# A warm-up that runs beside the first norm, and 2 KB rows for the input and the output of a recurrent mixer gated by routed experts

## The chip, the cores and the metric

The kernel runs on one core of a Trainium2 chip. TensorE (PE) multiplies matrices out of SBUF into PSUM banks, VectorE (DVE) and ScalarE (ACT) do the elementwise work, GpSimd (POOL) and SyncE (SP) mostly issue DMAs. Engines wait for each other and for DMAs by semaphores. The metric is the device time of one execution in microseconds (us); lower is better. Times of the kernel before are the median, the lowest and the highest of three runs; the profile is of one further execution.

## The reference, cut to what matters

The input x has 16 sequences of 256 tokens with 128 channels each, 4096 tokens in all, in float32.

```
xn   = (x - mean) / sqrt(var + 1e-5)                      # over the 128 channels of a token
s    = mixer(xn)       # shift by one token, six 128x128 projections, a scan over the 256 tokens,
                       # group norm over 8 channels, a gate, an output projection
cur  = xn
for r in range(4):                                        # four rounds of a mixture of experts
    logits = cur @ Wg[r] + bg[r]                          # 4 experts, the best 2 get a softmax weight cw
    hmid   = gelu(cur @ W1[e] + b1[e])                    # 128 -> 512, for every e
    y      = hmid @ W2[e] + b2[e]                         # 512 -> 128
    cur    = cur + sum_e cw[e] * y[e]
out  = x + s * silu(cur)
```

Every step but the norm, the last product and the last sum works on channels as rows, that is on x transposed.

## The kernel before

**Layout.** The work is done in NB = 8 blocks of BLK = 512 tokens, two sequences each. The large tensors hold channels in partitions and tokens along them: `cur` [128, 4096] is the state of the expert rounds, `xn_t` the normed input of the mixer. x comes from HBM with tokens in partitions instead. `load_x(c)` (L220) brings block c as four tiles of 128 tokens: tile t, partition p holds token 128t + p, which gives DMA rows of 128 floats, 512 B. The same layout is used when x is read again for the last sum (`load_x_again`, L272), and for the output (`store`, L278, and the two halves of the last block at L307 and L478).

**Start.** SP issues the loads of x blocks 0 and 1, then the eight loads of W1 and W2 in turns, then x blocks 2 to 7. DVE takes statistics of blocks 0 and 1 (`norm_stats`, L508), and then a chain of 14 tiny instructions of 8 columns gives 1/std by Newton steps (`norm_spread`, `norm_root`). `link` (L487) raises the semaphore `dve_step` after an instruction whose result the next one reads, and makes DVE wait for it; that happens 15 times up to 1/std. Then DVE norms two tiles of block 0 (L773, raises `xn_first`), ACT the other two (`scale_block`, L357, raises `xn_ready`). Ahead of `scale_block(0)` ACT has four roundings of weights in its queue (L426 to L429), each of which waits for its load. PE turns the four tiles of block 0 by transposes with `turn_normed(0)` (L893): the stationary operand is the normed tile in `xn_st` (its memory is `o`), the moving one is the identity `ident`, and tile t lands in columns 128t to 128t + 127 of the bank `pb`. DVE splits the result in a high and a low part (`split_cur(0)`, L571 and L573), and PE begins `up(0)`, three matmuls of 512 columns for each of four banks (L887, L888, L891). ACT takes each bank by a GELU (L389).

**Warm-up.** PE has nothing to do until block 0 is normed. It runs WARM_UP = 52 transposes of the identity into a bank that nobody reads (L1012), and FILL = 4 more behind `turn_normed(0)` (L1015).

**Main part.** 128 steps (4 rounds, 8 blocks, 4 experts) follow. In each, PE does `up` of the next step and `down` of this one, 24 matmuls of 512 columns, and pieces of the mixer, of the router and of the norm of blocks 2 to 7 are put between by fixed tables of steps. POOL adds each expert's result to `cur` by an accumulating DMA (L329).

**End.** For blocks 0 to 6, once their last round is done, ACT and DVE form th = s·silu(cur) with channels in partitions, PE turns it back by `turn_product(b)` (L904, four transposes at L909, the stationary operand is a tile of `th`), DVE adds x (L762), and SP stores. The last block goes in two halves: two transposes each (L1053), two sums (L881), and one store from SP (L307) and one from ACT (L478).

Of the kernel before, what the change touches and what calls it, by code (L numbers as in the profile page):

```python
# [5 lines left out]
D = 128  # L6
# [15 lines left out]
RSQRT_SEED = float(0x5F3759DF)  # L22
WARM_UP, FILL = 52, 4
DMA = 16
# [45 lines left out]
def mixer_gated_experts(nc, x, proj_t, mixes, wout_t, chan_vecs, wg, bg, w1, b1, w2, b2, cw_scratch, out):  # L70
# [7 lines left out]
    with ExitStack() as ctx:  # L78
# [134 lines left out]
        def block_of(k):  # L213
            return slice(k % NB * BLK, (k % NB + 1) * BLK)

        block = ctx.enter_context(nc.Block())

        @block.sync
        def _(sp):
            def load_x(c):  # L220
                sp.dma_start(cur[:, block_of(c)].rearrange("p (t d) -> p t d", t=TPB),
                             x[c * BLK:(c + 1) * BLK, :].rearrange("(t p) d -> p t d", p=128)).then_inc(x_loaded[c], DMA)

# [48 lines left out]
            def load_x_again(b):  # L272
                if b >= 2:
                    sp.wait_ge(r_empty, r_jobs["end", b - 2] + 1)
                sp.dma_start(xr[:, b % 2, :].rearrange("p (t d) -> p t d", t=TPB),
                             x[b * BLK:(b + 1) * BLK, :].rearrange("(t p) d -> p t d", p=128)).then_inc(x_again[b % 2], DMA)

            def store(b):  # L278
                sp.wait_ge(r_empty, r_jobs["end", b] + 1)
                sp.dma_start(out[b * BLK:(b + 1) * BLK, :].rearrange("(t p) d -> p t d", p=128),  # L280
                             o[:, b % 2, :].rearrange("p (t d) -> p t d", t=TPB)).then_inc(stored[b % 2], DMA)

# [17 lines left out]
            for b in range(NB - 1):  # L300
# [3 lines left out]
                if END_TURN + 2 + b < TURNS:  # L304
                    spread_gates(END_TURN + 2 + b)
            sp.wait_ge(half_done, 1)
            sp.dma_start(out[(NB - 1) * BLK:(NB - 1) * BLK + BLK // 2, :].rearrange("(t p) d -> p t d", p=128),  # L307
                         o[:, 1, 0:BLK // 2].rearrange("p (t d) -> p t d", t=TPB // 2)).then_inc(last_stored, DMA)
# [23 lines left out]
        def _(act):  # L332
# [139 lines left out]
            for n in range(2):  # L472
# [4 lines left out]
            act.wait_ge(half_done, 2)  # L477
            act.dma_start(out[(NB - 1) * BLK + BLK // 2:NB * BLK, :].rearrange("(t p) d -> p t d", p=128),  # L478
                          o[:, 1, BLK // 2:BLK].rearrange("p (t d) -> p t d", t=TPB // 2)).then_inc(last_stored, DMA)
# [405 lines left out]
        def _(pe):  # L885
# [7 lines left out]
            def turn_normed(b):  # L893

                if b == 0:
                    pe.wait_ge(xn_first, 1)
                else:
                    pe.wait_ge(p_empty, b)
                pe.wait_ge(xn_ready, b + 1)
                for t in range(TPB):  # L900
                    ins = nc.tensor.transpose(pb[:, t * D:(t + 1) * D], xn_st[:, b % 2, t * D:(t + 1) * D], ident[:, :])
                ins.then_inc(p_full, 1)

            def turn_product(b):  # L904

                pe.wait_ge(z_ready, b + 1)
                pe.wait_ge(r_empty, r_jobs["end", b])
                for t in range(TPB):
                    ins = nc.tensor.transpose(rb[:, t * D:(t + 1) * D], th[:, b % 2, t * D:(t + 1) * D], ident[:, :])  # L909
                ins.then_inc(r_full, 1)  # L910
# [100 lines left out]
            for _ in range(WARM_UP):  # L1011
                nc.tensor.transpose(rb[:, 0:D], ident[:, :], ident[:, :])  # L1012
            turn_normed(0)
            for _ in range(FILL):
# [34 lines left out]
            for n in range(2):  # L1049
                pe.wait_ge(half_z, n + 1)  # L1050
                for t in range(2):
                    col = n * HALF + t * D
                    ins = nc.tensor.transpose(hb[n][:, t * D:(t + 1) * D], th[:, (NB - 1) % 2, col:col + D], ident[:, :])  # L1053
                ins.then_inc(half_turned, 1)
# [33 lines left out]
```

## Time and profile before

| what | value |
|---|---|
| three timed runs | 809.54 us median (808.49 to 809.75) |
| the profiled execution's own time | 809.94 us |
| its span, first to last instruction | 808.1 us |
| PE / DVE / ACT / POOL busy | 98% / 88% / 81% / 14% |
| mean granted clock of TensorE | 0.995 of full |

The span and the device time of the same execution differ by 1.8 us, which lies before the first and behind the last instruction. Idle time of an engine that is not the bottleneck costs nothing; the busy share of PE counts modelled ends of overlapping matmuls, so it says that PE rarely stops and not how fast it goes. Where PE's speed matters, the granted clock of the stretch and the distance from one matmul's start to the next are read.

### The profile page before, as it was taken

The page shows a single profiled execution, that of the slowest core. Times are in us where ns is not written, and L with a number is a line of the kernel's source. Part 1 is how long each engine was busy: PE and PEld are TensorE (multiplying, and loading weights), DVE is VectorE, ACT ScalarE, POOL GpSimd, SP SyncE. Part 2 cuts the span into 40 slices and gives each one's busy share as a digit, 9 for nine tenths or more (in the row PEclk, how much of TensorE's full clock was granted, in tenths as well). Part 3 has the DMA queues.
Part 4 walks back from the last instruction along what each step waited for, and adds up shares of the span by engine and source line. Part 5 has one row for each costly group of instructions (what it writes and reads, how often), then busy time and mean ns, then how long its engine had stood idle before and what let it go on. Part 6 is the DMA issues. An engine that isn't in the chain of part 4 may idle for free.

```text
span 808.1 us, 10652 instructions
## 1 busy us (share of the span) xinstructions
PE 794.2 (98%) x3668; PEld 639.0 (79%) x3668; DVE 712.0 (88%) x1328; ACT 652.7 (81%) x912; POOL 114.5 (14%) x135
## 2 busy tenths in 40 slices
PE   7999999999999999999999999999999999999997
PEld 6778788887888878888788887888788887777885
DVE  5989888889998989889998899898989898989887
ACT  6899888877888877888787887788788887778775
POOL 0021111111111111111111101111111111011110
PEclk9999999999999999999999999999999999999998
DMA  9444462432532416333264322544235343264532
GB/s 256 121 84 123 81 183 54 105 92 40 147 83 59 104 27 158 93 72 73 40 145 105 92 40 56 134 108 96 41 90 133 92 117 77 40 172 105 130 66 52
DMA packets 44468, 78.50 MB, mean 97 GB/s; under 512 B 6656, under 2 KB 23552, under 8 KB 40448
## 3 DMA queue, kind: packets, MB, share of 16 engines
q0 software_dynamic: 18144, 33.04, 24.3%
q1 hardware_dynamic: 25136, 44.64, 16.5%
q8 instruction: 29, 0.48, 0.2%
q10 hardware_dynamic: 1136, 0.16, 0.1%
q14 instruction: 23, 0.19, 0.1%
HBM read 40.34 MB, written 2.36 MB: 53 GB/s over the span
## 4 chain that ended last, share of the span: by engine, by line
PE 91%; DVE 3%; DMA 3%; ACT 1%; issue 1%; SPq 0%; DVEq 0%; ACTq 0%; POOLq 0%
PE h_bank L887 14%; PE h_bank L891 14%; PE y_bank L952 14%; PE y_bank L948 14%; PE y_bank L947 14%; PE h_bank L888 14%; DMA cur<-tmp 2%; PE p_bank L887 2%; PE p_bank L891 2%; PE p_bank L888 2%; PE r_bank L986 1%; PE p_bank L917 1%; DMA cw_b<-in_w 1%; DVE g_lo L624 1%; ACT g L389 1%
## 5 line engine op out<-in xcount | busy, mean ns | idle before, releaser
L389 ACT ACTIVATE g<-h_bank,b_c 128x512 f32<-128x512 f32 x512 | 330.0, 682 | 75.0 <-PE h_bank L891 73.4
L624 DVE TENSOR_TENSOR g_lo<-g,g_hi 128x1024 fp32r<-128x1024 f32 x256 | 308.4, 1221 | 64.9 <-ACT g_hi L393 64.2
L393 ACT ACTIVATE g_hi<-g 128x1024 fp32r<-128x1024 f32 x256 | 271.9, 1062 | 8.1
L329 POOL DMA_DIRECT2D cur<-tmp x126 | 113.3, 899 | 680.9 <-DVE tmp L638 546.3
L887 PE MATMUL h_bank<-cur_hi,w_hi 128*128 128x512 f32 x512 | 206.5, 403 | 0.6 <-ACT g L389 0.4
L891 PE MATMUL h_bank<-cur_lo,w_hi 128*128 128x512 f32 x512 | 203.9, 398 | 0.0
L888 PE MATMUL h_bank<-cur_hi,w_lo 128*128 128x512 f32 x512 | 202.8, 396 | 0.0
L947 PE MATMUL y_bank<-g_hi,w_hi 128*128 128x512 f32 x508 | 201.1, 396 | 0.0
L948 PE MATMUL y_bank<-g_hi,w_lo 128*128 128x512 f32 x508 | 200.6, 395 | 0.0
L952 PE MATMUL y_bank<-g_lo,w_hi 128*128 128x512 f32 x508 | 139.3, 396 | 0.0
L891 PEld LDWEIGHTS h_bank<-cur_lo,w_hi 128*128 128x128 f32 x512 | 96.4, 188 | 23.4 <-DVE cur_lo L573 0.2
L887 PEld LDWEIGHTS h_bank<-cur_hi,w_hi 128*128 128x128 f32 x512 | 97.0, 189 | 21.6 <-issue 2.2
L947 PEld LDWEIGHTS y_bank<-g_hi,w_hi 128*128 128x128 f32 x508 | 95.4, 188 | 23.5 <-issue 0.8
L948 PEld LDWEIGHTS y_bank<-g_hi,w_lo 128*128 128x128 f32 x508 | 95.4, 188 | 23.2
L952 PEld LDWEIGHTS y_bank<-g_lo,w_hi 128*128 128x128 f32 x508 | 95.4, 188 | 22.9
L888 PEld LDWEIGHTS h_bank<-cur_hi,w_lo 128*128 128x128 f32 x512 | 96.7, 189 | 19.1
L638 DVE SCALAR_TENSOR_TENSOR tmp<-y_bank,b_c,cw_b 128x512 f32<-128x512 f32 x127 | 94.4, 743 | 1.3 <-DMA cur<-tmp 1.2
L672 DVE SCALAR_TENSOR_TENSOR xm<-xx,mix,xn_t 128x256 f32<-128x256 f32 x96 | 42.0, 479 | 0.6
L680 DVE TENSOR_TENSOR xm_lo<-xm,xm_hi 128x512 fp32r<-128x512 f32 x48 | 33.2, 692 | 1.7
L887 PE MATMUL p_bank<-xm_hi,pj_hi 128*128 128x256 f32 x96 | 27.3, 285 | 0.0
L891 PE MATMUL p_bank<-xm_lo,pj_hi 128*128 128x256 f32 x96 | 27.2, 283 | 0.0
L888 PE MATMUL p_bank<-xm_hi,pj_lo 128*128 128x256 f32 x96 | 27.0, 282 | 0.0
(133 smaller groups left out, 497.5 us busy)
## 6 DMA issues: line engine op xcount, KB each, us to landing
cur<-tmp POOLq DMA_DIRECT2D x126, 256.0 KB, 3.4
cw_b<-cw_scratch SPq DMA_DIRECT2D x31, 1024.0 KB, 5.1
cur<-in_x SPq DMA_DIRECT2D x8, 256.0 KB, 5.6
xn_t<-cur SPq DMA_DIRECT2D x8, 256.0 KB, 2.9
xr<-in_x SPq DMA_DIRECT2D x8, 256.0 KB, 3.5
out<-o SPq DMA_DIRECT2D x7, 256.0 KB, 2.4
cw_b<-in_w SPq DMA_DIRECT2D x4, 256.0 KB, 6.2
cw_b<-cw_scratch SPq DMA_DIRECT2D x1, 768.0 KB, 5.4
```

Of the source, the lines that this page charges most:

```text
L329: pool.dma_start(cur[:, block_of(s // E)], tmp[:, s % 2, :], accum_op=ALU.add).then_inc(summed, DMA)
L389: nc.scalar.activation(g[:, gb, ft * BLK:(ft + 1) * BLK], hb[ft][:, :], ACT.Gelu_apprx_tanh, bias=b1_c[:, e * FT + ft:e * FT + ft + 1]).th ...
L393: nc.scalar.activation(g_hi[:, gb, h], g[:, gb, h], ACT.Copy).then_inc(g_hi_done, 1)
L624: nc.vector.tensor_tensor(g_lo[:, gb, h], g[:, gb, h], as_f32(g_hi[:, gb, h]), ALU.subtract).then_inc(g_lo_done, 1)
L638: nc.vector.scalar_tensor_tensor(out=tmp[:, s % 2, :], in0=yb[s % 2][:, :], scalar=b2_c[:, e:e + 1], in1=cw_b[:, q, e * BLK:(e + 1) * BLK] ...
L672: last = nc.vector.scalar_tensor_tensor(out=xm[:, n, :], in0=xx[:, :], scalar=mix[:, k:k + 1], in1=xs[:, 1:LEN + 1], op0=ALU.mult, op1=ALU ...
L887: nc.tensor.matmul(out_ap, w_hi, v_hi, start=True, stop=False)
L888: nc.tensor.matmul(out_ap, w_lo, v_hi, start=False, stop=False)
L891: return nc.tensor.matmul(out_ap, w_hi, v_lo, start=False, stop=True)
L947: nc.tensor.matmul(yb[b][:, :], w2_hi[:, e * FT + ft, :], hi, start=(ft == 0), stop=False)
L948: nc.tensor.matmul(yb[b][:, :], w2_lo[:, e * FT + ft, :], hi, start=False, stop=False)
L952: last = nc.tensor.matmul(yb[b][:, :], w2_hi[:, e * FT + ft, :], g_lo[:, b, ft * BLK:(ft + 1) * BLK], start=False, stop=(ft == FT - 1))
```

## The change

There are two parts.

**Tokens per partition.** `by_partition` and `by_tile` give every DMA of x and of the output another split: partition p of a block holds tokens 4p to 4p + 3, so that one DMA row is 2 KB. In the last block, which is stored in halves, partition p holds two neighbouring tokens of each half, 1 KB rows. Tile t of a block now holds the tokens t, t + 4, t + 8 and so on. So that `cur` and `xn_t` keep tokens in order, `turn_normed` writes each tile into every fourth column of the bank (every second column of a half in the last block), and `turn_product` and the last turns read every fourth (second) column of `th` as stationary operand. `tokens_of` gives these slices. The four transposes of a block, and their sizes, stay.

**Warm-up.** The 52 transposes become 36, then 15 pairs, each behind a wait for one of DVE's 15 steps up to 1/std, then 3 behind the wait for `xn_first`: 69 in all. The 4 of FILL stay.

```diff
-WARM_UP, FILL = 52, 4
+WARM_UP, FILL = 36, 4
+
+ROOT_CHAIN = 15
...
+        def by_partition(b, rows):
+            if b < NB - 1:
+                return rows.rearrange("(p t) d -> p t d", t=TPB)
+            return rows.rearrange("(n p t) d -> p n t d", n=2, t=TPB // 2)
+
+        def by_tile(b, ap):
+            if b < NB - 1:
+                return ap.rearrange("p (t d) -> p t d", t=TPB)
+            return ap.rearrange("p (n t d) -> p n t d", n=2, t=TPB // 2)
+
+        def tokens_of(b, t):
+
+            if b < NB - 1:
+                return slice(t, BLK, TPB)
+            n, i = t // (TPB // 2), t % (TPB // 2)
+            return slice(n * HALF + i, (n + 1) * HALF, TPB // 2)
...
-                sp.dma_start(cur[:, block_of(c)].rearrange("p (t d) -> p t d", t=TPB),
-                             x[c * BLK:(c + 1) * BLK, :].rearrange("(t p) d -> p t d", p=128)).then_inc(x_loaded[c], DMA)
+                sp.dma_start(by_tile(c, cur[:, block_of(c)]),
+                             by_partition(c, x[c * BLK:(c + 1) * BLK, :])).then_inc(x_loaded[c], DMA)
...
-                sp.dma_start(out[b * BLK:(b + 1) * BLK, :].rearrange("(t p) d -> p t d", p=128),
-                             o[:, b % 2, :].rearrange("p (t d) -> p t d", t=TPB)).then_inc(stored[b % 2], DMA)
+                sp.dma_start(by_partition(b, out[b * BLK:(b + 1) * BLK, :]),
+                             by_tile(b, o[:, b % 2, :])).then_inc(stored[b % 2], DMA)
...
-                    ins = nc.tensor.transpose(pb[:, t * D:(t + 1) * D], xn_st[:, b % 2, t * D:(t + 1) * D], ident[:, :])
+                    ins = nc.tensor.transpose(pb[:, tokens_of(b, t)], xn_st[:, b % 2, t * D:(t + 1) * D], ident[:, :])
...
-                    ins = nc.tensor.transpose(rb[:, t * D:(t + 1) * D], th[:, b % 2, t * D:(t + 1) * D], ident[:, :])
+                    ins = nc.tensor.transpose(rb[:, t * D:(t + 1) * D], th[:, b % 2, tokens_of(b, t)], ident[:, :])
...
             for _ in range(WARM_UP):
+                nc.tensor.transpose(rb[:, 0:D], ident[:, :], ident[:, :])
+            for n in range(ROOT_CHAIN):
+                pe.wait_ge(dve_step, n + 1)
+                for _ in range(2):
+                    nc.tensor.transpose(rb[:, 0:D], ident[:, :], ident[:, :])
+            pe.wait_ge(xn_first, 1)
+            for _ in range(3):
                 nc.tensor.transpose(rb[:, 0:D], ident[:, :], ident[:, :])
             turn_normed(0)
...
-                    ins = nc.tensor.transpose(hb[n][:, t * D:(t + 1) * D], th[:, (NB - 1) % 2, col:col + D], ident[:, :])
+                    ins = nc.tensor.transpose(hb[n][:, t * D:(t + 1) * D], th[:, (NB - 1) % 2, tokens_of(NB - 1, 2 * n + t)],
+                                              ident[:, :])
```

`load_x_again` changes like `load_x`, and the two half stores of the last block change from `"(t p) d -> p t d"` to `"(p t) d -> p t d"` with t = 2.

PE's queue at the start of the program, before. L1012 is the warm-up, L901 the turn of block 0, L1015 FILL, L887 to L891 the first bank of `up(0)`.

```order
L1012 MATMUL r_bank<-ident 128x128 [waits made]
L1012 MATMUL r_bank<-ident 128x128 x51
L901 MATMUL p_bank<-ident,o 128x128 [waits xn_ready,xn_first]
L901 MATMUL p_bank<-ident,o 128x128 x3
L1015 MATMUL r_bank<-ident 128x128 x4
L887 MATMUL h_bank<-cur_hi,w_hi 128x512 [waits cur_split,w1_low]
```

The same place now (the pair at L1036 stands 15 times, two of them are shown; lines have moved by 20 and more).

```order
L1032 MATMUL r_bank<-ident 128x128 [waits made]
L1032 MATMUL r_bank<-ident 128x128 x35
L1036 MATMUL r_bank<-ident 128x128 [waits dve_step]
L1036 MATMUL r_bank<-ident 128x128
L1036 MATMUL r_bank<-ident 128x128 [waits dve_step]
L1036 MATMUL r_bank<-ident 128x128
...
L1039 MATMUL r_bank<-ident 128x128 [waits xn_first]
L1039 MATMUL r_bank<-ident 128x128 x2
L921 MATMUL p_bank<-ident,o 128x128 [waits xn_ready,xn_first]
L921 MATMUL p_bank<-ident,o 128x128 x3
L1042 MATMUL r_bank<-ident 128x128 x4
L907 MATMUL h_bank<-cur_hi,w_hi 128x512 [waits cur_split,w1_low]
```

The turn of block 0 stands behind 69 transposes instead of 52, the last 33 of them behind waits for DVE.

SP's queue at the start, before; the shape is partitions x tiles x floats of a row.

```order
L221 DMA cur<-in_x 128x4x128 x2
L225 DMA cw_b<-in_w 128x512 x2
L228 DMA th<-in_w 128x4x128
L225 DMA cw_b<-in_w 128x512
```

And now.

```order
L241 DMA cur<-in_x 128x512 x2
L245 DMA cw_b<-in_w 128x512 x2
L248 DMA th<-in_w 128x4x128
L245 DMA cw_b<-in_w 128x512
```

The order of SP's queue is the same; a load of x is 128 rows of 512 floats where it was 512 rows of 128.

## Rows read from the trace of the kernel before

**Rows 1.** The page, span and PE's busy share.

```profile
span 808.1 us, 10652 instructions
...
PE 794.2 (98%) x3668; PEld 639.0 (79%) x3668; DVE 712.0 (88%) x1328; ACT 652.7 (81%) x912; POOL 114.5 (14%) x135
```

**Rows 2.** Chain that ended last, 0 to 19 us: start, us, what.

```profile
3.26 6.56 DMA cw_b<-in_w
...
10.47 0.78 ACT o L365 x2
...
11.39 0.64 PE p_bank L901 x4
...
12.05 0.70 DVE cur_hi L571
...
14.51 0.43 PE h_bank L887
...
16.39 0.23 PE h_bank L887
...
17.09 0.45 PE p_bank L901 x4
...
18.68 0.58 ACT g L389
```

**Rows 3.** Timeline of ACT, 5 to 22 us: start, us, instruction, idle before.

```profile
9.85 0.63 ACT L345 ACTIVATE w_hi<-cw_b 128x512 fp32r<-128x512 f32 x1
...
14.25 0.58 ACT L374 ACTIVATE cur<-p_bank 128x512 f32<-128x512 f32 x1
14.73 0.67 ACT L389 ACTIVATE g<-h_bank,b_c 128x512 f32<-128x512 f32 x1
15.73 0.69 ACT L389 ACTIVATE g<-h_bank,b_c 128x512 f32<-128x512 f32 x1 [0.33 <-PE h_bank L891]
```

**Rows 4.** Timeline of DVE, 5 to 15 us.

```profile
5.97 0.87 DVE L513 BATCH_NORM_STATS2 stats<-cur 128x6 f32<-128x128 f32 x4 [1.32 <-DMA cur<-in_x]
...
9.95 0.17 DVE L533 SCALAR_TENSOR_TENSOR shift<-mean,rstd 128x8 f32<-128x8 f32 x1
...
12.78 0.69 DVE L573 TENSOR_TENSOR cur_lo<-p_bank,cur_hi 128x512 fp32r<-128x512 f32 x1
```

**Rows 5.** Timeline of PE, 0 to 14 us.

```profile
1.77 7.56 PE L1012 MATMUL r_bank<-ident 128*128 128x128 f32 x52 [1.77 <-POOL ident L318]
11.39 0.63 PE L901 MATMUL p_bank<-ident,o 128*128 128x128 f32 x4 [2.06 <-ACT o L365]
```

**Rows 6.** Windows: busy of each engine, granted clock, DMA share, GB/s last.

```profile
4.00:5.00 1.00, 1.00 (x6) 1.00 (x5) 0.65 (x4) 1.00 (x1) 0.00 (x0) 1.00 0.88 109
5.00:6.00 1.00, 1.00 (x11) 1.00 (x10) 0.03 (x1) 0.31 (x2) 0.00 (x0) 1.00 0.81 276
...
12.00:13.00 1.00, 0.83 (x6) 0.46 (x3) 0.91 (x2) 1.00 (x4) 0.00 (x0) 0.52 1.22 290
13.00:14.00 1.00, 1.00 (x3) 0.76 (x4) 1.00 (x3) 1.00 (x3) 0.00 (x0) 0.50 1.23 290
...
5.20:9.60 4.40, 4.13 (x38) 3.89 (x36) 3.18 (x20) 1.89 (x4) 0.00 (x0) 1.00 1.08 330
```

**Rows 7.** The page, DMA issues: KB each, median us to landing.

```profile
out<-o SPq DMA_DIRECT2D x1, 128.0 KB, 1.9
```

**Rows 8.** Waits of PE, whole span: waited for, us in total, times, longest.

```profile
PE r_bank L909 <- DVE th L737: 4.1, 3, 1.5
```

**Rows 9.** Timeline and window of the end.

```profile
804.12 1.12 PE L1053 MATMUL h_bank<-ident,th 128*128 128x128 f32 x4 [2.56 <-DVE th L753]
804.94 0.76 DVE L881 TENSOR_TENSOR o<-h_bank,xr 128x256 f32<-128x256 f32 x2 [0.54 <-PE h_bank L1053]
...
803.00:806.00 3.00, 1.12 (x4) 0.67 (x4) 2.15 (x7) 0.42 (x1) 0.00 (x0) 0.66 0.00 0
```

More of the change, by code:

```diff
@@ L274, in load_x_again @@
                     sp.wait_ge(r_empty, r_jobs["end", b - 2] + 1)
-                sp.dma_start(xr[:, b % 2, :].rearrange("p (t d) -> p t d", t=TPB),
-                             x[b * BLK:(b + 1) * BLK, :].rearrange("(t p) d -> p t d", p=128)).then_inc(x_again[b % 2], DMA)
+                sp.dma_start(by_tile(b, xr[:, b % 2, :]),
+                             by_partition(b, x[b * BLK:(b + 1) * BLK, :])).then_inc(x_again[b % 2], DMA)
             def store(b):
                 sp.wait_ge(r_empty, r_jobs["end", b] + 1)
-                sp.dma_start(out[b * BLK:(b + 1) * BLK, :].rearrange("(t p) d -> p t d", p=128),
-                             o[:, b % 2, :].rearrange("p (t d) -> p t d", t=TPB)).then_inc(stored[b % 2], DMA)
+                sp.dma_start(by_partition(b, out[b * BLK:(b + 1) * BLK, :]),
+                             by_tile(b, o[:, b % 2, :])).then_inc(stored[b % 2], DMA)
             copy_block(0)
@@ L306, in _ @@
             sp.wait_ge(half_done, 1)
-            sp.dma_start(out[(NB - 1) * BLK:(NB - 1) * BLK + BLK // 2, :].rearrange("(t p) d -> p t d", p=128),
+            sp.dma_start(out[(NB - 1) * BLK:(NB - 1) * BLK + BLK // 2, :].rearrange("(p t) d -> p t d", t=TPB // 2),
                          o[:, 1, 0:BLK // 2].rearrange("p (t d) -> p t d", t=TPB // 2)).then_inc(last_stored, DMA)
@@ L477, in _ @@
             act.wait_ge(half_done, 2)
-            act.dma_start(out[(NB - 1) * BLK + BLK // 2:NB * BLK, :].rearrange("(t p) d -> p t d", p=128),
+            act.dma_start(out[(NB - 1) * BLK + BLK // 2:NB * BLK, :].rearrange("(p t) d -> p t d", t=TPB // 2),
                           o[:, 1, BLK // 2:BLK].rearrange("p (t d) -> p t d", t=TPB // 2)).then_inc(last_stored, DMA)
@@ L1051, in _ @@
                 for t in range(2):
-                    col = n * HALF + t * D
-                    ins = nc.tensor.transpose(hb[n][:, t * D:(t + 1) * D], th[:, (NB - 1) % 2, col:col + D], ident[:, :])
+                    ins = nc.tensor.transpose(hb[n][:, t * D:(t + 1) * D], th[:, (NB - 1) % 2, tokens_of(NB - 1, 2 * n + t)],
+                                              ident[:, :])
                 ins.then_inc(half_turned, 1)
```

## The prediction, written before the changed kernel ran

> **What bounds the kernel now.** I read the page first: PE is busy for 98% of 808.1 us [rows 1]. So in the main part nothing but PE's own work counts, and a change that leaves the matmuls alone can only win at the start, at the end, or where PE is seen to wait. The waits of PE give just one such place in between, 4.1 us over three turns of a finished block at L909 [rows 8]; it waits there for DVE's product, whose inputs come from the accumulating DMAs.
>
> Then I read the chain of the start. It runs through the loads of W1 until 9.8 us, through ACT's fourth rounding (9.85) and its first two normed tiles (10.47), to PE's turn of block 0 at 11.39, DVE's split at 12.05, `up(0)`, and ends up on ACT, whose third GELU at 18.68 releases PE [rows 2]. Three things stand out. DVE has 1/std and the shift at 9.95 + 0.17 = 10.12 [rows 4], before ACT is free, so ACT and the weight loads bind and not DVE's chain. From 9.85 on ACT works without a gap, save 0.33 us at 15.73 where it waits for PE [rows 3]. And PE idles for 2.06 us between warm-up and turn [rows 5], after which its granted clock reads 0.52 and 0.50 of full from 12 to 14 us, the lower of the two levels (1.2 GHz) [rows 6]; a matmul of 512 columns takes 0.43 us there and 0.23 us later [rows 2].
>
> **Warm-up, PE.** At the full clock four turns take 0.45 us, 0.11 each [rows 2]. At half the clock I take twice that, 0.22, as the big matmuls do (0.43 against 0.23). The 52 fit this: PE's records per us go from 6 to 11 between the windows 4 to 5 and 5 to 6 [rows 6], so the step lies near 5.2 us; (5.2 - 1.77) / 0.22 = 16 at 0.22, then 36 at 0.11 = 4.0, together 7.4 of 7.56 us [rows 5]. Now there are 69: 16 at 0.22 (3.4 us) and 53 at 0.11 (5.8 us), so PE's queue reaches the turn at 1.77 + 9.2 = 11.0 us at the earliest. The 36 end near 7.4. The first of DVE's 15 steps comes right behind the statistics, at 5.97 + 0.87 = 6.84, the last near 9.95 [rows 4], 0.22 apart, and a pair takes 0.22 too, so PE trails DVE closely and hardly waits. The gap of 2.06 us is gone, PE is busy up to the turn, and I expect the clock to stay at the higher level. What is queued behind these waits is the turn of block 0 alone; it begins at 11.0 instead of 11.39, -0.37, if ACT's tiles are there.
>
> What is that worth? DVE's split moves with the turn: the low part ends at 12.78 + 0.69 - 0.37 = 13.1. `up(0)` starts at 12.5, waits for the low part, and at 0.23 per matmul its second bank is ready near 14.0, long before ACT asks. So ACT's gap of 0.33 closes, with some hundredths of others, 0.4 us in all. From 18.68 on PE follows ACT, so 0.4 us is what the clock gives, and not the 0.2 us on each of ten matmuls at the lower level: ACT takes over as the bound.
>
> The Trainium skill, "TensorE: Matmul & The Clock Gate", Part 4 (PE-mode transpose), says that transposes do not count as PE activity for the clock in the way matmuls do. The trace disagrees: with nothing but transposes running, PE's records per us went from 6 to 11 and the clock of 5.2 to 9.6 us is 1.00 [rows 6]. By that rule the longer warm-up would hold nothing; this is the second rival below.
>
> **2 KB rows, loads at the start.** A load of x in 512 B rows runs at 290 GB/s where it is alone (13 to 14 us), while the stretch 5.2 to 9.6 us, mostly 2 KB rows of W1, reads 330 [rows 6]. For 256 KB that is 0.90 against 0.79 us, 0.11 per load, and two stand ahead of the weights: 0.2 us is the lower bound for how much sooner the weights land. Above: between 4 and 5 us the queues moved only 109 GB/s at a DMA share of 0.88 [rows 6], so the small packets of the second load (landed 5.97, [rows 4]) drag there; if blocks 0 and 1 passed at 330 GB/s from the first packet, the second would be in up to 2 us sooner. But ACT's use of it is capped: its copy of block 0 at 14.25 [rows 3] waits for the split, 13.1, so 1.15 us is the upper bound. I take 0.7, the middle, since I see both the drag and no reason that it goes in full. Then ACT's fourth rounding starts at 9.15, its two tiles are ready near 10.6, the turn starts at 11.0, where PE's queue arrives, and ACT reaches its copy at 13.55, behind the split. ACT's chain is 0.7 + 0.4 = 1.1 us earlier at 18.68, and PE with it for the rest of the run. Bounds: 0.6 to 1.55.
>
> **2 KB rows, middle.** Seven stores and eight second loads of x get cheaper for the DMA engines by 0.11 us each, on a queue with slack. They share the engines with the accumulating DMAs that PE's three waits (4.1 us, [rows 8]) hang on: fewer packets help, larger ones make the other queue wait longer for its turn. I take 0, with 0.5 us either way.
>
> **End.** The half store lands 1.9 us after issue [rows 7]. With 1 KB rows 128 KB gain at most 0.06 us by the rates above; I take 0.05. The clock is at 0.66 on the mean of 803 to 806 us [rows 9]: the last four turns, at 804.12, run at the lower level, 0.82 us before DVE's first sum. If the end shifts by 1.1 us some of this may run before the clock falls: 0 to 0.4 us, of which I take 0.15.
>
> **Strided turns.** This is the part that I can't read from the trace. 32 turns write every fourth PSUM column (28 in the running stream), 28 + 4 read every fourth or second column of `th`. No row shows a strided operand on PE. Below: nothing, because a turn takes 0.11 us for 128 columns and a matmul 0.23 us for 512 [rows 2], so a turn streams at half the rate per column that PE and PSUM manage, which leaves room for an access to twice as many lines. Above: half speed, 0.22 instead of 0.11, as at the low clock, so 0.11 on each of 64, 7.0 us (3.5 for writes alone, 3.5 for reads alone). I take 0, by that spare rate.
>
> The Trainium skill, "Advanced Engine Details and Errata", Memory Cachelines, says of PSUM that "Any non-contiguous AP significantly slows down matmuls", as its lines hold two floats, and of SBUF that one access per 16-byte line costs. A step of four floats is one access per line in both. No run here shows it. By that rule the writes and the reads would both slow, 7.0 us by the bound above.
>
> **Sum.** -1.1 (start) - 0.05 - 0.15 (end) = -1.3 us against the profiled execution, 809.94 to 808.6. The median of the timed runs is 0.4 us lower than that execution, so I forecast 808.2 us.
>
> **Rivals.**
> First, strided turns are slow. It decides from 0.05 us per turn (64 x 0.05 = 3.2, less 1.3, is beyond 1.6). If one side, writes or reads, goes at half speed: +3.5 - 1.3, 811.7 us; both: 815.2. For it speaks that nothing in the kernel so far strides on PE, against it the spare rate of a turn. It is slower than before.
> Second, the clock still falls near 12 us, because ACT's tiles come late, or warm-up transposes don't hold it. Then PE runs ten matmuls at 0.43 and bounds the start; only the turn's 0.37 is kept, plus 0.1 at the end: 809.1 us.
> Third, the warm-up itself is late. If the clock rises later than at 5.2 us in an execution, more of the 69 take 0.22: 16 more of them put the turn at 12.8, 1.4 us after 11.39, so the time is about 0.5 us above before, 810.0. The 52 of before would have been done by 11.1.
> Fourth, the drag on the second load was the small rows' doing and goes in full, and the end gains its 0.4: 1.55 + 0.45 = 2.0 us, 807.5.
>
> **Chances.** About 0.2%, 1.6 us, is what a measurement of this kernel can tell from no change. The forecast 0.35 (808.2, its own range 807.6 to 808.9), the fourth 0.22, the second 0.09, the third 0.06, strided turns 0.28. Faster by over 1.6 us: the fourth and a quarter of the forecast's, 0.31. Slower: the strided turns and a little, 0.29. Within: 0.40. The range runs from 807.2 to 812.5; it holds the forecast, the second and third, the fourth, and strided turns on one side only, and leaves out half speed on both sides.
>
> **What would show it.** PE's timeline: transposes without a gap above 0.3 us from 1.77 to about 11.0, then the turn; a clock of 1.00 in the windows from 12 to 16 us; if the gap stays away and the clock still falls, the warm-up step is wrong. DVE's second statistics start by 0.5 us or more before 5.97, and ACT's fourth rounding near 9.15; if it stays at 9.6 or later, the DMA step is wrong. ACT's third GELU of `up(0)`, at 18.68 in the chain, comes near 17.6. The chain's row for four turns at the full clock reads 0.45 us if strides are free, and up to 0.9 if not, for blocks 1 to 7, and likewise at the seven turns of the products. PE's waits at the products stay near 4.1 us. The forecast is wrong if turns slow by 0.05 us or more each, or if the start gains less than 0.6 us.

## The result: 812.06 us, slower by 0.4%

The changed kernel takes 812.06 us (median of 6, 811.45 to 813.66). The kernel before took 809.43 us in the median on the same chip (6 runs, 808.49 to 809.75). The ratio is 1.0038, with a 95% interval of 1.0027 to 1.0050; it follows the means of the runs, and the medians lie 2.6 us, 0.3%, apart. The forecast was 808.2 us and faster; the time lies in the range of 807.2 to 812.5, but on the other side of the kernel before. Single executions that ran far longer as a whole (one each in e5, in e16 and in the runs of the kernel before beside e13 to e16) are left out of the medians and ratios, and their traces are not read.

The profiled execution took 811.45 us, 1.5 us more than that of before (809.94), and its span is 1.5 us longer (809.65 against 808.14). The page of the changed kernel, beside [rows 1]:

```profile
span 809.7 us, 10686 instructions
...
PE 796.4 (98%) x3685; PEld 641.6 (79%) x3685; DVE 711.6 (88%) x1328; ACT 652.2 (81%) x912; POOL 114.5 (14%) x135
...
DMA packets 35637, 78.52 MB, mean 97 GB/s; under 512 B 6656, under 2 KB 12032, under 8 KB 31616
...
xr<-in_x SPq DMA_DIRECT2D x8, 256.0 KB, 2.8
out<-o SPq DMA_DIRECT2D x7, 256.0 KB, 2.0
```

The DMA part of the change does what it says: there are 35,637 packets where there were 44,468, a second load of x lands in 2.8 us instead of 3.5, and a store in 2.0 instead of 2.4. The kernel is slower all the same. Laying the starts of PE's matmuls of both traces side by side (after minus before) says where:

```
at us    +us    place (times of the kernel before)
 11.4   +0.92   first turn of block 0
 15.5   -0.08   third bank of up(0); +0.02 at 694, behind the first turns of products
716.8   +1.2    PE stops for ACT's GELU
719.9   +1.6    turn of a finished product
795.3   +1.9    behind the last turns of products
804.1   +1.9    first half turn
804.6   +1.75   third half turn; span +1.5
```

So there are four readings: the start, the stretch 702 to 722 us, the turns and the end.

**The start.** PE's timeline of the changed kernel, as in [rows 5] (start, us, instruction, idle before):

```profile
1.77 7.10 PE L1032 MATMUL r_bank<-ident 128*128 128x128 f32 x36 [1.77 <-POOL ident L338]
8.70 3.44 PE L1036 MATMUL r_bank<-ident 128*128 128x128 f32 x30
11.98 0.49 PE L1039 MATMUL r_bank<-ident 128*128 128x128 f32 x3
12.30 0.60 PE L921 MATMUL p_bank<-ident,o 128*128 128x128 f32 x4
```

The gap is gone, but the 36 took 7.10 us where I had 5.6, and the turn starts at 12.30. The windows (PE, PEld, DVE, ACT, POOL, granted clock, DMA share, GB/s; compare [rows 6]):

```profile
5.00:6.00 1.00, 1.00 (x7) 1.00 (x6) 0.47 (x3) 0.13 (x1) 0.00 (x0) 1.00 0.65 209
...
12.00:13.00 1.00, 1.00 (x12) 1.00 (x11) 0.06 (x1) 1.00 (x4) 0.00 (x0) 1.00 1.07 373
13.00:14.00 1.00, 0.56 (x5) 0.35 (x3) 0.97 (x2) 1.00 (x3) 0.00 (x0) 1.00 1.05 385
```

Between 5 and 6 us PE still does 7 transposes per us, not 11: in this execution the clock came to its full level at 7.85 us, against 5.22 before. (The column of the granted clock reads 1.00 here all the same: the trace's record of the clock begins only when it rises, so before that PE's rate has to be read.) From 12 to 14 us it is 1.00 where it was 0.52 and 0.50, so the longer warm-up does hold it. The loads of x run at 373 and 385 GB/s against 290. DVE and ACT, as in [rows 3, 4]:

```profile
5.53 0.88 DVE L533 BATCH_NORM_STATS2 stats<-cur 128x6 f32<-128x128 f32 x4 [1.21 <-DMA cur<-in_x]
...
9.50 0.17 DVE L553 SCALAR_TENSOR_TENSOR shift<-mean,rstd 128x8 f32<-128x8 f32 x1
...
9.89 0.63 ACT L365 ACTIVATE w_hi<-cw_b 128x512 fp32r<-128x512 f32 x1
...
15.01 1.33 ACT L409 ACTIVATE g<-h_bank,b_c 128x512 f32<-128x512 f32 x2
```

The second block of x is in 0.44 us sooner (5.53 against 5.97), but ACT's fourth rounding starts at 9.89, no sooner than the 9.85 of before: ACT, which bound here before, got nothing from the loads, and PE's 69 transposes, without a gap up to the turn, now come in last. The gap of 0.33 us between its first two GELUs is gone, and the late turn has taken it back.

**The stretch 702 to 722 us.** The chain of waits of the changed kernel, 711 to 724 us:

```profile
703.51 7.92 DMA cur<-tmp
...
711.96 4.73 DMA cur<-tmp
...
717.21 3.56 DMA cur<-tmp
720.78 0.68 DVE th L757
...
721.50 0.75 PE r_bank L929 x4
```

and that of the kernel before, which the prediction had not read:

```profile
703.55 7.45 DMA cur<-tmp
...
711.53 3.55 DMA cur<-tmp
...
715.62 3.55 DMA cur<-tmp
719.16 0.69 DVE th L737
...
719.90 0.66 PE r_bank L909 x4
```

Here the path runs over three accumulating DMAs in a row, not over PE. The first takes 0.47 us longer, the second 1.18 us, the third the same; less the 0.04 by which the stretch began sooner, that is the whole 1.6 us at the turn. The first of them stands beside another broadcast, issued at 704.0, a store and a second load of x. What stands beside the second is seen in SP's queue. The timeline of the changed kernel:

```profile
706.22 0.32 SPq L283 DMA_DIRECT2D cw_scratch<-cw  x1
711.96 0.86 POOL L349 DMA_DIRECT2D cur<-tmp  x1 [7.59 <-DMA cur<-tmp]
712.72 0.32 SPq L290 DMA_DIRECT2D cw_b<-cw_scratch  x1
716.71 0.63 ACT L444 ACTIVATE th<-cur 128x512 f32<-128x512 f32 x1 [4.20 <-DMA cur<-tmp]
```

and of the kernel before:

```profile
706.26 1.14 SPq L263 DMA_DIRECT2D cw_scratch<-cw  x1
711.53 0.86 POOL L329 DMA_DIRECT2D cur<-tmp  x1 [7.12 <-DMA cur<-tmp]
712.69 0.33 SPq L270 DMA_DIRECT2D cw_b<-cw_scratch  x1
715.11 0.64 ACT L424 ACTIVATE th<-cur 128x512 f32<-128x512 f32 x1 [2.65 <-DMA cur<-tmp]
```

The gates' save (L283, before L263) is issued at 706.2 in both, and the broadcast of the gates (1 MB in 8 KB rows), which waits in SP's queue for the save to land, at 712.7 in both. The accumulate, issued when the one before it has landed, comes 0.43 us later in the changed kernel. So the broadcast follows it after 0.76 us instead of 1.16. The records of the DMA packets show what that does. In the kernel before, 101 of the accumulate's 128 packets of 2 KB start before 714 us and the others before 715, and the 8 KB packets begin behind 714. In the changed kernel 49 start before 714 us, 47 before 715, and 32 later, when 8 KB packets (42 in that us, 324 ns each) already hold the engines. The sum lands late, so does the tanh (wait 4.20 instead of 2.65), and PE stops twice:

```profile
PE r_bank L929 <- DVE th L757: 4.4, 3, 1.9
...
PE h_bank L907 <- ACT g L409: 1.3, 2, 0.9
```

These are PE's waits (us in total, times, longest); [rows 8] had 4.1 for the first, and the wait of 0.9 us for the GELU is new.

**The turns.** Read by form, the instructions of the two turn lines (ns, least/median/most):

```profile
L929 PEld LDWEIGHTS r_bank<-ident,th x28: 195/211/220, 642.2 to 797.0; 128*128 128x128 f32 x28
L929 PE MATMUL r_bank<-ident,th x28: 270/285/386, 642.4 to 797.1; 128*128 128x128 f32 x28
...
L921 PE MATMUL p_bank<-ident,o x32: 270/272/273, 12.3 to 84.4; 128*128 128x128 f32 x32
```

and of the product's turns before:

```profile
L909 PEld LDWEIGHTS r_bank<-ident,th x28: 137/141/142, 642.3 to 795.1; 128*128 128x128 f32 x28
L909 PE MATMUL r_bank<-ident,th x28: 270/273/328, 642.5 to 795.2; 128*128 128x128 f32 x28
```

Writing every fourth PSUM column costs nothing: 272 ns, one per 0.109 us as before. Reading every fourth column of `th` costs something: the weight load takes 211 ns instead of 141, and the turns follow each other at 0.122 us instead of 0.109. That is 28 x 0.013 = 0.4 us.

**The end**, as in [rows 7, 9]:

```profile
806.00 0.96 PE L1079 MATMUL h_bank<-ident,th 128*128 128x128 f32 x4 [2.56 <-DVE th L773]
806.65 0.78 DVE L901 TENSOR_TENSOR o<-h_bank,xr 128x256 f32<-128x256 f32 x2 [0.37 <-PE h_bank L1079]
...
805.00:806.00 1.00, 0.00 (x0) 0.00 (x0) 1.00 (x4) 0.39 (x1) 0.00 (x0) 1.00 0.00 0
806.00:807.00 1.00, 0.96 (x4) 0.64 (x4) 0.63 (x3) 0.00 (x0) 0.00 (x0) 0.78 0.00 0
```

DVE's sum starts 0.65 us behind the first half turn instead of 0.82: part of the turn still runs at the full clock. The forecast had 0.15 for this, and it is 0.17. The half stores land in 1.7 us instead of 1.9, for which the forecast had 0.05. Together the end is 0.4 us shorter: 1.9 us late before the half turns, 1.5 in the span.

### The profile page after: what moved, and what is told of

Same layout as the page of the kernel before. It is cut to its first block, busy times and chain, and to the rows that moved or that the text cites. A ratio compares the mean times of both kernels' runs of the same rounds, so it can differ in the third digit from the quotient of the medians.

```text
span 809.7 us, 10686 instructions
## 1 busy us (share of the span) xinstructions
PE 796.4 (98%) x3685; PEld 641.6 (79%) x3685; DVE 711.6 (88%) x1328; ACT 652.2 (81%) x912; POOL 114.5 (14%) x135
## 2 busy tenths in 40 slices
DMA packets 35637, 78.52 MB, mean 97 GB/s; under 512 B 6656, under 2 KB 12032, under 8 KB 31616
## 4 chain that ended last, share of the span: by engine, by line
PE 92%; DVE 3%; DMA 2%; ACT 1%; issue 1%; POOL 0%; DVEq 0%; POOLq 0%; ACTq 0%
PE y_bank L972 14%; PE h_bank L911 14%; PE h_bank L907 14%; PE y_bank L968 14%; PE y_bank L967 14%; PE h_bank L908 14%; DMA cur<-tmp 2%; PE p_bank L907 2%; PE p_bank L911 2%; PE p_bank L908 2%; PE r_bank L1006 1%; PE r_bank L1032 1%; PE p_bank L937 1%; DVE g_lo L644 1%; ACT g L409 1%
```

## The experiments

Ratios are to the kernel before, run in turn with each on the same chip; they follow the means, so the medians can give a ratio that is some hundredths of a per cent away. Five rounds unless it says otherwise.

**Halves of the change.** The warm-up alone:

```diff
-WARM_UP, FILL = 52, 4
+WARM_UP, FILL = 36, 4
+            for n in range(ROOT_CHAIN):
+                pe.wait_ge(dve_step, n + 1)
+                (two transposes)
+            pe.wait_ge(xn_first, 1), and three more
```

> The kernel before with the new warm-up alone (36, 15 pairs behind DVE's steps, 3), old layout. Theory A (the loss sits in the DMAs around the finished blocks, near 704 to 720 us): no loss here, within 0.4 us of before, 809.0 to 809.8; the part of the chain behind 20 us is unchanged. Theory B (the 69 transposes put the first turn late when the clock rises late, as in the profile after, 7.85 us and a turn at 12.3): 0.3 to 1.5 us slower than before.

Measured: 809.26 against 809.28 us, 1.0000 [0.9991, 1.0009]. The profiled execution took 808.43 us, and here the clock rose at 5.02 us:

```profile
10.92 0.60 PE L902 MATMUL p_bank<-ident,o 128*128 128x128 f32 x4
...
8.96 0.63 ACT L346 ACTIVATE w_hi<-cw_b 128x512 fp32r<-128x512 f32 x1
...
4.00:5.00 1.00, 1.00 (x6) 1.00 (x5) 0.70 (x4) 1.00 (x1) 0.00 (x0) 1.00 0.83 158
```

In this execution everything came as predicted for the clock: the 36 transposes took 5.71 us, the turn came at 10.92, the third GELU at 17.22. And the fourth rounding came at 8.96 with the 512 B rows of before, whose queues moved 158 GB/s between 4 and 5 us instead of 109. When the loads at the start let ACT begin this rounding differs by 0.9 us from execution to execution with the same rows.

The layout alone, all of the diff but the warm-up:

> The changed kernel with the old warm-up of 52. Theory A: as slow as the changed kernel, 811.5 to 812.5, with PE's waits near 717 us 1.0 to 1.5 us longer than before. Theory B: 809 to 809.8 (a load 0.4 us sooner, strided reads +0.4 us), the changed kernel's loss gone.

Measured: 812.93, 1.0051 [1.0033, 1.0068]. The whole loss is in the layout. Next its two sides: 2 KB rows in the first loads with strided PSUM writes (e3), and the rest: second loads, stores and strided reads of `th` (e4).

> Only the first loads of x in 2 KB rows, with the strided PSUM writes of the turns; second loads, stores, turns of the products and warm-up as before. Theory A: no loss, 809.0 to 809.6; turns of blocks 1 to 7 still 0.45 us per four. If strided writes cost: 3.5 us slower.

Measured: 809.08, 1.0000 [0.9992, 1.0009]; turns at 0.109 us. The input's side costs and gives nothing.

> Only the second loads of x and the stores in 2 KB rows, with the strided reads of th in the turns; first loads and warm-up as before. Theory A: the loss is here, 811 to 812, of it 0.4 us from strided reads (0.12 instead of 0.11 us per turn) and the rest at the wait near 717 us. Theory B: 809.5 to 810, only the reads' 0.4 us.

Measured: 812.6, 1.0035 [1.0021, 1.0049]. All of it is in the output's side. The chain of e4 has the second accumulate at 5.78 us:

```profile
711.36 5.78 DMA cur<-tmp
...
717.66 3.54 DMA cur<-tmp
```

PE's stop there is 2.1 us, and behind it the granted clock falls (e4's windows; columns as above):

```profile
718.00:719.00 1.00, 0.59 (x2) 0.50 (x3) 0.00 (x0) 0.97 (x3) 0.52 (x1) 0.75 0.00 0
719.00:722.00 3.00, 2.34 (x7) 1.34 (x5) 1.94 (x3) 2.97 (x5) 0.00 (x0) 0.51 0.52 90
```

e2's profiled execution (815.38 us) shows the same from 722.7 to 726.1 us, beside a fall at the start as in the kernel before. This is a second price of the late sum, paid in some executions only; in the profiled execution of the change the clock stayed up. How far it lifts the median of the change is not shown. The traces in which the clock falls once have a mean granted clock of 0.995 or 0.996, those in which it does not 0.998 or 0.999; of the six executions of the change two have 0.995 and less, and the two at the median have 0.997.

**Rows or reads?** e5 keeps the 2 KB rows of e4 and turns `th` by contiguous columns; e6 keeps the strided reads with the rows of before. Both leave out the right order of the output's tokens.

```diff
e5 -  ... th[:, b % 2, tokens_of(b, t)]      e6 -  by_tile / by_partition in load_x_again, store, last stores
   +  ... th[:, b % 2, t * D:(t + 1) * D]       +  "(t p) d -> p t d" as before
```

> Second loads and stores in 2 KB rows, but the turns of the products read th contiguously, so that rows of the output stand at other tokens (the order of the output is left out). Theory A1 (2 KB packets of SP's queue set the accumulating DMA near 711 us against the broadcast of the gates): all but 0.4 us of the loss of e4 is here, 811.5 to 812.5; tanh near 715 us waits 4 to 5.4 us for its accumulate instead of 2.7. Theory A2 (the strided reads of th make the loss): 809.0 to 809.6.

> DMAs as before, only the turns of the products read th in steps of four, two in the last block (the order of the output is left out). Theory A1: 0.3 to 0.5 us over before (28 turns at 0.122 instead of 0.109 us), 809.5 to 809.9. Theory A2: 811.5 to 812.5.

Measured: e5 811.5, 1.0036 [1.0023, 1.0048]; e6 811.05, 1.0026 [1.0017, 1.0035]. The rows alone make a loss as large as e4's, within the intervals. That the reads also seem to make 2.1 us did not fit e6's own trace, in which the turns cost 0.4 us and the span is 807.3; so it was tried again (e15). The kernel of e5 was run once more for its trace:

> The kernel of e5 once more, for a trace (the order of the output is left out): tanh of block 3 waits 4 us or more for its accumulate, the broadcast is issued 0.6 to 0.9 us behind the accumulate instead of 1.16, and turns of the products stay at 0.109 us; 811 to 812.5.

Measured, one run: 812.1 us, span 810.3, turns at 0.109 us, in its chain the second accumulate at 4.93 us, and a clock that falls at 721.9 us for 3.4 us. The rows do it without any strided read.

**The broadcast held back.** If the 8 KB packets between those of the accumulate are the cause, the change with the broadcast issued behind the accumulate must lose nothing:

```diff
+                if k == 29:
+                    sp.wait_ge(summed, DMA * 112)
                 sp.dma_start(cw_b[:, q, rest], line[rest].partition_broadcast(128)).then_inc(cwb_ready[q], DMA)
```

> The changed kernel, with one wait more on SP: the broadcast of the gates of turn 29 starts only when the accumulate that the tanh of block 3 waits for has landed (summed at 112). Theory A1: the loss goes, 808.8 to 810.0; tanh near 715 us waits 2.9 us or less, the clock does not fall there. If the delay is not from that collision: no change, 811.5 to 812.7, or slower if the broadcast becomes late itself.

Measured: 809.57 (11 runs, 809.16 to 809.9), 1.0007 [0.9998, 1.0016]. Its chain and SP's queue:

```profile
711.42 3.29 DMA cur<-tmp
...
714.74 0.64 ACT L446 ACTIVATE th<-cur 128x512 f32<-128x512 f32 x1 [2.99 <-DMA cur<-tmp]
714.78 0.32 SPq L292 DMA_DIRECT2D cw_b<-cw_scratch  x1
```

The accumulate lands in 3.29 us, the tanh comes at 714.74, the GELU's wait of 0.9 us is gone, and with it the loss: the medians lie 0.6 us above the kernel before on the same chip (809.57 against 808.97) where the change's lay 2.6 above. Of the 0.6 the strided reads make 0.4. None of the 11 executions has a mean clock under 0.997. One wait of one DMA for another, everything else as in the change, so it is shown that the loss hangs on the broadcast beside the second accumulate. The first accumulate still takes 8.15 us here.

**Stores or loads?** With three rounds each, the kernel before with 2 KB rows in the stores alone, or in the second loads alone (the order of tokens in the output is left out):

> The kernel before with only the stores of the output in 2 KB (1 KB in the last block) rows; second loads and turns as before (the order of the output is left out). By the collision theory each of the two, store and second load, brings the broadcast nearer to the accumulate by about half: 1.16 us apart becomes 0.95, and the loss lies between: 809.5 to 811.5.

> The kernel before with only the second loads of x in 2 KB rows (the order of the output is left out). The second load's packets are the last of SP's queue ahead of the gates' save, so if only one of the two matters it is this one: 810.5 to 812, and e13 at 809.3. If both count by half: 809.5 to 811.5.

Measured: stores 811.39, 1.0021 [1.0011, 1.0031]; loads 810.79, 1.0015 [1.0006, 1.0024]. Their chains have the second accumulate at 4.00 and 3.86 us instead of 3.53 to 3.56, so each brings on a part of the collision. That is 0.3 to 0.5 us, and with the stores the first accumulate is 0.2 to 0.5 us longer too; the medians lie 2.2 and 1.6 us above before. Most of it is the second price. In both profiled executions PE's stop at the turn of the product is 1.87 us, where it is 1.5 to 1.7 us in before, e1 and e3, and behind it the clock falls for 3.4 us. e14's window (columns as above):

```profile
720.00:723.00 3.00, 3.00 (x10) 2.25 (x9) 2.93 (x6) 2.39 (x4) 0.86 (x1) 0.53 0.00 0
```

Laid beside e3, whose clock stays up, e14's matmuls are 0.1 us late when this turn begins, 1.6 us late at 723.4 us, and 1.7 at the end. 8 of e14's 10 executions and 7 of e13's 8 have a mean clock of 0.996 or less.

The two differ in how they bring the broadcast nearer. With the stores the first accumulate takes 7.97 us (old rows: 7.45 to 7.74), and the broadcast follows the second after 0.86 us; with the loads it takes 7.48, but the broadcast comes sooner, 9.0 us behind the first accumulate's issue instead of 9.1 to 9.4, and follows the second after 1.01. The lengths of the two accumulates in the kernels without a held broadcast (us), by the chain, with the gap from the second's issue to the broadcast's:

```
kernel                          first          gap            second
before, e1, e3, e6, e8, e15     7.45 to 7.74   1.16 to 1.18   3.53 to 3.56
e14 (2 KB in the loads)         7.48           1.01           3.86
e13 (2 KB in the stores)        7.97           0.86           4.00
e2 (2 KB in both)               7.82           0.80           4.50
after                           7.92           0.76           4.73
e12                             7.99           0.74           4.93
e4                              8.04           0.69           5.78
```

The second accumulate grows as the gap shrinks, without an exception. With the old rows the first accumulate differs by 0.3 us from trace to trace too, but the broadcast moves with it and the gap stays.

**The reads again**, with the new warm-up:

> Strided reads of th as in e6, with the new warm-up of 36 + 30 + 3 (the order of the output is left out). If strided reads cost only what the trace shows, 0.4 us: 809.3 to 809.9 and a span 0.4 us over that of e1. If they cost the 2 us of e6's median: 811 or more. A clock that falls at the start in e6 (5 of 11 at a mean of 0.995) can't fall here.

Measured: 809.69, 1.0003 [0.9994, 1.0013], spans 807.85 in the median against 807.4. The strided reads cost some 0.4 us, as their rows say. The chain has the accumulates at 7.71, 3.56 and 3.56 us, as before: reads do not touch them. So e6's 2.1 us are not the reads'. Its six executions with a mean clock of 0.997 or 0.998 have a median span of 807.5 us, against 807.2 for the 25 such executions of the kernel before beside it, which is about what the reads cost. The rest is of two kinds: five of its 11 executions have a mean clock of 0.995, as those in which the clock falls once, and its times lie 2.6 us above their spans in the median instead of 1.8. Why e6 had more of both than e15 is open. (In e2 and e4 the distance to the span is also up to 2.8 us.)

**A shorter warm-up.** 18 instead of 36, on e1:

```diff
-WARM_UP, FILL = 36, 4
+WARM_UP, FILL = 18, 4
```

> The kernel before with the new warm-up, 18 transposes ahead of the 15 pairs instead of 36. Theory W (the 69 transposes arrive late, near 12.3 us, in the executions where the clock rises late, and in time where it rises early; that is why the warm-up alone gave nothing in the median): 0.5 to 1.0 us faster than before in the median, 808.3 to 808.8, and a narrower spread. If it is not the length: 809.2 as with 36.

Measured: 809.26 against 808.97, 1.0010 [1.0001, 1.0018]. With the clock up at 6.12 us the turn came at 11.17, not much before that of e7 (6.18, 11.49), and DVE and ACT bind again: no gain. The profiled execution took 810.99 us, and its clock fell too, at 719.5 us for 3.4 us, behind a stop of 1.81 us:

```profile
719.00:723.00 4.00, 3.65 (x11) 3.07 (x12) 3.93 (x8) 3.35 (x5) 0.86 (x1) 0.57 0.00 0
```

Its DMAs are those of the kernel before, so the fall in the middle does not need the 2 KB rows. 3 of its 11 executions have a mean clock of 0.995, and 1 of e1's 11 has 0.996.

**Holding the broadcasts in the other kernels.** If the kernel before also pays for the crowd, a wait before broadcasts 28 and 29 should gain there (e9), with the warm-up and the input's rows (e10), and in the change (e11):

```diff
+                if k in (28, 29):
+                    sp.wait_ge(summed, DMA * (k + 83))
```

> The kernel before, with the broadcasts of the gates of turns 28 and 29 held until the accumulates 111 and 112 have landed. If the crowd of DMAs costs time before the change too (tanh waits 2.65 us there, PE 1.5 us at 720): accumulate 111 lands near 707 instead of 711, PE's wait at 720 shrinks by 0.5 to 1.5 us, no execution with the clock fallen there; 808.0 to 808.6. If that wait has another cause: 808.9 to 809.3, no change.

> New warm-up, first loads in 2 KB rows, old second loads and stores, and both broadcasts held as in e9. Sum of the parts that gained or cost nothing: e9's time less 0.3 to 0.8 us from the start, 807.4 to 808.3; if start and crowd gain nothing, 809.0.

> The changed kernel with both broadcasts held. By the collision theory the 2 KB rows cost nothing once nothing collides: 0.4 us (strided reads) above e10, 808.0 to 809.2, and under e7's 809.6. If 2 KB rows hurt elsewhere: as e7 or above.

Measured against 810.02: e9 810.1, 1.0003 [0.9994, 1.0012]; e10 809.51, 0.9995 [0.9986, 1.0004]; e11 810.0, 1.0001 [0.9993, 1.0010]. Nothing is gained. e9's chain says why:

```profile
703.49 3.25 DMA cur<-tmp
...
707.27 8.10 DMA cur<-tmp
```

Without the broadcast beside it the first accumulate takes 3.25 us instead of 7.45. But that broadcast, issued at 706.8 us now, stands beside the second, which takes 8.10 us instead of 3.55, and DVE begins the product at 719.45 us instead of 719.16. PE's wait at the products falls from 4.1 to 2.9 us, and a new one of 0.9 us appears at the mixer's projections, for `xm_hi`, which DVE makes behind the product. The three together also say what the 2 KB rows cost once the broadcasts are held: e11 lies 0.5 us above e10, and the strided reads alone make 0.4 of it.

**The best of it**: input rows, warm-up of 18, broadcast 29 held, output as before.

> What gained or cost nothing, together: first loads in 2 KB rows, warm-up of 18 + 30 + 3, old second loads and stores, the broadcast of turn 29 held as in e7. 0.3 to 1.0 us faster than before if start and clock gains add up; equal if the held broadcast costs what they bring.

Measured: 809.0 against 809.2, 0.9997 [0.9988, 1.0006]. No version beats the kernel before by what can be measured.

## Why the prediction was wrong, step by step

**The step that failed is "2 KB rows, middle"**, taken at 0 with 0.5 us either way. I had named the effect, that larger packets make the other queue wait longer, and its size on the accumulate beside the store and the load is 0.47 us, at the bound that I gave. (Between traces with the same old rows this accumulate differs by 0.3 us, so 0.47 is not all the rows' doing.) What the step left out is the next one: an accumulate that is issued 0.4 us later meets the broadcast of the gates, whose own time did not move, and takes 1.18 us more. Together 1.6 us in the profiled execution, and about 1.5 more where the clock falls behind the stop (e14 beside e3). That the broadcast is the second part's cause is shown (e7), that the rows of stores and loads bring it on as well (e12, e13, e14). Why the first accumulate takes longer beside 2 KB rows than beside 512 B rows is not shown. [rows 8] showed that PE waits at the products; the chain of waits at 703 to 720 us, which I did not read, shows that for 16 us the path is three accumulates in a row, so that what delays one of them is paid in full.

**Warm-up**: the mechanism was right. The clock stays at its higher level (1.00 in the windows from 12 us on, and none of the seven traces with the new warm-up shows a fall at the start), and it rose at 7.85 us after nothing but transposes. The Trainium skill ("TensorE: Matmul & The Clock Gate", Part 4) says that transposes do not count as PE activity in the way matmuls do; these traces disagree. By the rule the longer warm-up would have held nothing. What the old warm-up loses was read from one trace: of the nine traces with it only three (before, e2, e9) show the fall near 12 us, so the gain of 0.4 us was there to be had in a part of the executions. What was mis-sized is the time at which the clock rises. I took 5.2 us from one execution; the same warm-up gives:

```
kernel   clock up   turn of block 0   third GELU
e1         5.02         10.92           17.22
e7         6.18         11.49           17.81
e11        7.11         11.94           18.24
e10        7.34         12.05           18.37
e15        7.59         12.18           18.48
after      7.85         12.30           18.61
```

The turn comes 0.49 us later for each us of late clock, since transposes take 0.22 instead of 0.11 us until then: this is the third rival's mechanism, to which I gave 0.06. Five of these six traces show it. Its price was too high: with the turn at 12.30 the third GELU comes at 18.61, where the rival had a time 0.5 us above before for a turn at 12.8. Before had its third GELU at 18.68 with a clock that rose early and fell again, and over its 23 executions beside e1 the spans lie at 806.4 to 807.6 us (13, mean clock 0.997 or more, median 806.9) or at 807.4 to 808.8 (10, mean clock 0.995 or 0.996, as where the clock falls once). The new warm-up takes away most of the second group, and a late turn lengthens the first: e1's ten executions with the higher clock have a median span of 807.45. Median for median, nothing.

**Loads at the start**, -0.7: mis-sized. The second load is in 0.44 us sooner in the profiled execution, and that is mostly luck: the six traces with the new rows at the start have 5.29 to 5.73 us for the second statistics (median 5.65), the ten with the old ones 5.25 to 5.98 (median 5.77). ACT's fourth rounding comes at 9.11 to 10.08 us with the new rows and at 8.96 to 9.85 with the old ones, 9.6 in the median of both. The drag at 4 to 5 us that I charged half to the small rows differs between executions of the same rows (109 GB/s in before, 158 in e1). e3 puts the whole step at 0.0 with 0.7 us either way.

**Strided turns**: writes at 0, right. Reads at 0, too low by 0.4 us; the upper bound of 3.5 was far off, and the first rival did not come, although its number for one side (811.7) is near the result. The Trainium skill's rule ("Advanced Engine Details and Errata", Memory Cachelines) is half borne out: that PSUM's non-contiguous patterns slow matmuls is not so for these transposes (272 ns either way); that one access per 16-byte line costs in SBUF fits, by 211 against 141 ns for the weight load, most of which lies beside the matmul before.

**End**: -0.2 in the forecast, -0.4 in the trace. The clock's part is right (0.17 against 0.15); the half stores gained 0.2 us, where I had put 0.06 as the most.

By the steps, then: start -0.1 instead of -1.1, middle +1.6 instead of 0, reads +0.4 instead of 0, end -0.4 instead of -0.2: that is the +1.5 us of the span. The medians lie a further 1.1 us apart. 0.5 of it is that the profiled execution of before was a slow one of its kind (809.94 against a median of 809.43), and 0.6 that the profiled one of the change was its fastest (811.45 against 812.06). What the second part comes from is open. The clock behind the stop, which no step had, is one candidate: two of the change's six executions have a mean clock as low as the traces in which it falls, but the two at the median do not.

## What to carry to other kernels

Where small transfers follow each other on the path, a change of the packets beside them can delay one by some tenths and push the next into a large transfer that comes at its own time. Ask what is due behind it, and let the large one wait for the small one. Where PE is at 98%, read the chain of waits over each of its few waits, not the sum of the waits alone: if three DMAs follow each other there, their neighbours in other queues are part of the path.

A time taken from one execution (here when the clock rises, and when the first loads land) is no constant; a warm-up that is counted in instructions takes longer the later the clock rises, so its length is to be judged by the latest rise and not by the one profiled. (The shorter one tried here, e8, gained nothing either.)

## What was not expected of the hardware

- A 256 KB accumulate takes 3.5 us in this chain (3.53 to 3.56 in six kernels) with a 1 MB broadcast in 8 KB rows issued 1.16 to 1.18 us behind it, 3.9 to 5.8 with 0.7 to 1.0 us, and 3.25 to 3.29 where the broadcast was held until it had landed (e7, e9 to e11). A shift of 0.4 us in one queue cost 1.2 us in the other.
- The clock can fall in the middle of the run for 3.4 us, once PE goes on behind a stop: in e4 (stop of 2.09 us; 0.51 from 719 to 722 us), e14 (1.87) and e8 (1.81, with the DMAs of before). It stayed at 1.00 in before (1.52), e1 and e3 (1.69 each), and also in the change, where PE stopped for 0.94 and then for 1.87 us. Beside e3 it cost e14 1.5 us.
- Loads of x in 2 KB rows ran at 373 to 387 GB/s from 12 to 14 us (the change, e3), against 289 to 291 in rows of 512 B (before, e4).
- A transposing weight load that reads every fourth fp32 column takes 211 ns instead of 141, and the turns run at 0.122 us instead of 0.109; writing every fourth column of PSUM is free.
